# Transposing the query and key stacks of two heads at once

## What is computed

```python
x = x + 0.5 * ffn(layernorm(x))      # silu(x Wg^T) * (x Wu^T), then Wd^T; hidden 2048
q, k = unit_norm(q), unit_norm(k)    # per head; rotary embedding on every second head
logits = einsum(q, k) * q_gain       # causal mask, softmax
x = x + (softmax(logits) @ v) @ w_out
x = x + 0.5 * ffn(layernorm(x))
```

## Time and profile before

| | us |
|---|---|
| median of 3 runs | 2894.09 (2892.12 to 2894.12) |
| the profiled execution | 2897.56 |
| its span | 2895.8 |
| PE busy | 2765.8 (96%) |
| DVE busy | 1773.8 (61%) |
| ACT busy | 1193.0 (41%) |
| POOL busy | 535.8 (19%) |

### The profile page before, as it was taken

The page is one execution under the profiler, slowest core; times in us unless marked ns, Lnnn a source line. Parts: engine busy times, 40 slices in busy tenths (PEclk is TensorE's granted clock), DMA queues, the critical chain, the costliest instruction groups (busy, mean ns, idle before and its releaser), DMA issues.

```text
span 2895.8 us, 56172 instructions
## 1 busy us (share of the span) xinstructions
PE 2765.8 (96%) x23232; PEld 2029.6 (70%) x23232; DVE 1773.8 (61%) x4156; ACT 1193.0 (41%) x2218; POOL 535.8 (19%) x820
## 2 busy tenths in 40 slices
PE   4699989999999999999999999999999999998899
PEld 4467666777767776777767777677767777676676
DVE  8655766656566565666656666565656656566643
ACT  5233544444433443344433445344433443445422
POOL 0103122112030311203012131212103030123100
PEclk8899999999999999999999999999999999999999
DMA  6000000000000000000000000000000000000000
GB/s 249 15 1 1 1 1 1 16 1 16 1 1 16 16 1 1 1 16 16 1 1 1 16 16 2 1 16 9 9 1 1 16 16 1 1 1 9 1 9 15
DMA packets 15486, 37.28 MB, mean 13 GB/s; under 512 B 1408, under 2 KB 1408, under 8 KB 14720
## 3 DMA queue, kind: packets, MB, share of 16 engines
q1 hardware_dynamic: 15232, 33.70, 3.2%
HBM read 25.31 MB, written 8.39 MB: 12 GB/s over the span
## 4 chain that ended last, share of the span: by engine, by line
PE 84%; DVE 10%; ACT 3%; issue 2%; POOL 1%; DMA 0%; SPq 0%; DVEq 0%; ACTq 0%
PE psum L906 24%; PE psum L908 24%; PE psum L907 24%; PE psum L1055 2%; PE psum L1032 2%; PE psum L1067 1%; DVE mneg L820 1%; PE psum L1014 1%; DVE arena L841 1%; PE psum L949 1%; PE psum L1010 1%; DVE arena L768 1%; DVE arena L770 1%; PE psum L1033 1%; DVE arena L763 1%
## 5 line engine op out<-in xcount | busy, mean ns | idle before, releaser
L906 PE MATMUL psum<-arena,WG 128*128 128x256 f16 x2048 | 559.9, 273 | 1.4 <-DVE arena L763 1.4
L908 PE MATMUL psum<-arena,WG 128*128 128x256 f16 x2048 | 559.8, 273 | 0.0
L907 PE MATMUL psum<-arena,WG 128*128 128x256 f16 x2048 | 559.6, 273 | 0.0
L906 PE MATMUL psum<-arena,WU 128*128 128x256 f16 x2048 | 559.1, 273 | 0.0
L908 PE MATMUL psum<-arena,WU 128*128 128x256 f16 x2048 | 558.8, 273 | 0.0
L907 PE MATMUL psum<-arena,WU 128*128 128x256 f16 x2048 | 558.8, 273 | 0.0
L768 DVE SCALAR_TENSOR_TENSOR arena<-arena,psum 128x256 f32<-128x256 f32 x512 | 214.8, 420 | 529.1 <-ACT arena L643 528.1
L643 ACT ACTIVATE arena<-psum,tscale 128x256 f32<-128x256 f32 x512 | 241.8, 472 | 671.8 <-PE psum L908 671.7
L906 PE MATMUL psum<-WD,arena 128*128 128x512 f16 x1024 | 388.6, 379 | 12.7 <-DVE arena L774 12.7
L908 PE MATMUL psum<-WD,arena 128*128 128x512 f16 x1024 | 388.5, 379 | 0.0
L907 PE MATMUL psum<-WD,arena 128*128 128x512 f16 x1024 | 388.4, 379 | 0.0
(11 more groups left out here) (139 smaller groups left out, 4543.1 us busy)
## 6 DMA issues: line engine op xcount, KB each, us to landing
arena<-in_L_attn_x SPq DMA_DIRECT2D x16, 512.0 KB, 3.6
out<-arena SPq DMA_DIRECT2D x16, 512.0 KB, 2.8
arena<-in_L_ffn_w_gate SPq DMA_DIRECT2D x4, 1024.0 KB, 9.2
arena<-in_L_ffn_w_up SPq DMA_DIRECT2D x4, 1024.0 KB, 8.3
WD<-in_L_ffn_w_down SPq DMA_DIRECT2D x4, 1024.0 KB, 10.6
arena<-in_L_attn_w_qkv SPq DMA_DIRECT2D x1, 3072.0 KB, 20.6
WQ<-in_L_attn_w_out SPq DMA_DIRECT2D x1, 1024.0 KB, 22.8
ropet<-rope_table SPq DMA_DIRECT2D x1, 128.0 KB, 2.1
```

The source lines that it names most:

```text
L906: T_.matmul(o, lhs(0), rhs(0), start=first, stop=False)
L907: T_.matmul(o, lhs(0), rhs(1), start=False, stop=False)
L908: return T_.matmul(o, lhs(1), rhs(0), start=False, stop=last)
```

## The change

The query stack of a head is now written as (high, low) only, and the key stack as (low, high): 64 columns a head, so that two heads fill 128. One transpose turns two heads, 4 for the queries and 4 for the keys of a tile. In PSUM the even head lies on partitions 0 to 63 and the odd one on 64 to 127. Out of PSUM each group of four heads (even, odd) is copied twice: both parts to partitions 0 to 63 of QT or KT, and the high part once more to partitions 64 to 95. A query column is then (high, low, high) and a key column (low, high, high), which gives the same three products. One ScalarE instruction writes the high parts of all stacks.

```diff
-    STK = halves("work", 5 * D, HH * ST).rearrange("p (h c) -> p h c", h=2 * HH)
+    stk = halves("work", 5 * D, (2 * D + 2 * HD) // 2)
+    STQ, STK = (stk[:, D * a:D * (a + 1)].rearrange("p (h c) -> p h c", h=HH) for a in range(2))
+    SThi = stk.rearrange("p (a c) -> p a c", a=2)[:, :, 0:D].rearrange("p a (h c) -> p a h c", c=2 * HD)[:, :, :, 0:HD]
...
+    def stacked(key, odd):
+        bank = ps16(2 + key)[:, 0:D].rearrange("p (h n) -> p h n", n=P)
+        first = 2 * HD * odd
+        return bank[first + HD * key:first + HD * key + HD], bank[first:first + 2 * HD]
...
-                nc.scalar.activation(STK[:, :, 0:HD], q3, ACT.Copy)
-                nc.scalar.activation(STK[:, 0:HH, HD:2 * HD], q3[:, 0:HH, :], ACT.Copy)
-                nc.scalar.activation(STK[:, HH:2 * HH, 2 * HD:ST], q3[:, HH:2 * HH, :], ACT.Copy).then_inc(s["st_hi"], 1)
+                nc.scalar.activation(SThi, q3.rearrange("p (a h) c -> p a h c", a=2), ACT.Copy).then_inc(s["st_hi"], 1)
...
-                nc.scalar.activation(QT[0:ST, :, t * P:(t + 1) * P], ps16(2)[0:ST, :].rearrange("p (h n) -> p h n", h=HH),
-                                     ACT.Copy).then_inc(s["qt_ev"], 1)
+                for odd in range(2):
+                    high, both = stacked(0, odd)
+                    nc.scalar.activation(QT[0:2 * HD, odd::2, t * P:(t + 1) * P], both, ACT.Copy)
+                    ins = nc.scalar.activation(QT[2 * HD:ST, odd::2, t * P:(t + 1) * P], high, ACT.Copy)
+                ins.then_inc(s["qt_ev"], 1)
...
-                V_.tensor_copy(KT[0:ST, :, t * P:(t + 1) * P], ps16(3)[0:ST, :].rearrange("p (h n) -> p h n", h=HH)).then_inc(s["kt_ev"], 1)
+                for odd in range(2):
+                    high, both = stacked(1, odd)
+                    V_.tensor_copy(KT[0:2 * HD, odd::2, t * P:(t + 1) * P], both)
+                    ins = V_.tensor_copy(KT[2 * HD:ST, odd::2, t * P:(t + 1) * P], high)
+                ins.then_inc(s["kt_ev"], 1)
...
-                for h in range(HH):
-                    ins = T_.transpose(ps16(2)[0:ST, h * P:(h + 1) * P], STK[:, h, :], ident16[:, :])
+                for m in range(HH // 2):
+                    ins = T_.transpose(ps16(2)[:, m * P:(m + 1) * P], stk[:, m * P:(m + 1) * P], ident16[:, :])
...
-                for h in range(HH):
-                    ins = T_.transpose(ps16(3)[0:ST, h * P:(h + 1) * P], STK[:, HH + h, :], ident16[:, :])
+                for m in range(HH // 2):
+                    ins = T_.transpose(ps16(3)[:, m * P:(m + 1) * P], stk[:, D + m * P:D + (m + 1) * P], ident16[:, :])
```

More of the change, by code:

```diff
@@ L806, in stack @@
                 q3 = qn[t % 2].rearrange("p (h c) -> p h c", c=HD)
-                V_.tensor_tensor(STK[:, 0:HH, 2 * HD:ST], q3[:, 0:HH, :], STK[:, 0:HH, 0:HD], ALU.subtract)
-                V_.tensor_tensor(STK[:, HH:2 * HH, HD:2 * HD], q3[:, HH:2 * HH, :], STK[:, HH:2 * HH, 0:HD], ALU.subtract).then_inc(s["st_lo"], 1)
+                V_.tensor_tensor(STQ[:, :, HD:2 * HD], q3[:, 0:HH, :], STQ[:, :, 0:HD], ALU.subtract)
+                V_.tensor_tensor(STK[:, :, 0:HD], q3[:, HH:2 * HH, :], STK[:, :, HD:2 * HD], ALU.subtract).then_inc(s["st_lo"], 1)
             def stack_out(b, hf, t):
                 wait("kt_ps", tile_no(b, hf, t) + 1)
-                V_.tensor_copy(KT[0:ST, :, t * P:(t + 1) * P], ps16(3)[0:ST, :].rearrange("p (h n) -> p h n", h=HH)).then_inc(s["kt_ev"], 1)
+                for odd in range(2):
[3 more added lines that the diff above has]
+                ins.then_inc(s["kt_ev"], 1)
             mnegv = mneg[:, :].rearrange("p (t h) -> p t h", t=TT)
```

## The result

The changed kernel takes 2905.95 us (median of 6 runs, 2903.62 to 2908.93) against 2894.11 before (6 runs): ratio 1.0041, 95% interval 1.0031 to 1.0052. It is 11.8 us slower, where 6.7 was forecast (2901, range 2884 to 2908).

A forecast was written before the change was run, and what follows sets the result against it. PE, with 84% of the chain that ended last, was taken as the bound, so new PE waits count. 6.6 lost in batches 1 to 6 plus 0.1 in batches 0 and 7 gave 6.7 slower: 2901 median, range 2884 to 2908.

The forecast's parts named there:

- the forecast's own case: All new copies on ACT and DVE held until the one before is done: 6.7 slower, 2901; chance 0.55.
- two of the rivals: ACT held in part or not, 2894 (chance 0.17), wholly in range; copies overlapping, 2883 (chance 0.18), at its edge.
- Transposes, 0.44 a tile: PE: 8 transposes replace 16 at 0.056 each, 28 us over 64 tiles if nothing else moved.
- Copies held at each change of partition: Four PSUM copies per engine, each waiting for its predecessor: ACT ends at +2.86 (before +1.67), DVE +2.42 (before +1.79).
- The rivals of overlap, on both engines or on ACT alone: Copies overlap on both engines: 2883, chance 0.18; ACT held in part or not, DVE fully: 2894, chance 0.17.
- Single rate: DVE copies on 64 or 32 partitions lose the double rate, 0.69 a copy: 2937; chance 0.05.
- Tile by tile: Batches 1 to 6: losses and gains at each tile's PE waits sum to 1.10 lost a batch, 6.6 in six.
- `scores max` at +2.96: t3: waits for the query copies; 0.75 lost in half 0, 0.41 in half 1.
- `down` at +3.88: t2, both halves: waits for L774, late behind the query copies and L649; +3.51 before, 0.37 lost each.
- `turn` at +2.52: t0 of half 0: L949 needs the key copies; +2.20 before, 0.32 lost.
- Batches 0 and 7: 0.1 give or take 3: First and last batch: 0.7 and 2.7 lost, 1.2, 0.7 and 1.4 gained, 0.1 lost in sum.
- a gain of 0.7: Fourth `scores max` of batches 0 and 7, behind 2677.26 at low clock: its 16 transposes take 1.73 and become half.

The follow-up runs named there:

- half_transposes: Kernel before, with only 4 of the 8 query and 4 of the 8 key transposes per tile, copies kept at full size: 2870.94 against 2893.55, ratio 0.9924.
- split_heads: Kernel before, each copy out of PSUM made in four by heads, all of 96 partitions from and to partition 0: 2897.69, ratio 1.0015.
- split_partitions: Kernel before with its 16 transposes, each copy out of PSUM made in four with the changed kernel's sizes and partition changes: 2938.56, ratio 1.0157.
- queries_only: Kernel before with the change on the queries alone (4 transposes, four ACT copies), keys as before: 2904.54, ratio 1.0040.
- before_order: Kernel before, in half 0 last stack turn one fill earlier, feed-forward parts ahead of the copies and of unit: 2894.43, ratio 0.9995.
- sbuf_keys: Changed kernel with the keys' high parts copied the second time within SBUF instead of out of PSUM: 2898.05, ratio 1.0008.

## Why the prediction was right, and where it was too small

The measured 2905.95 lies in the stated range and in the narrower one of the forecast's own case (2897 to 2907), 5 above the forecast. The stated range takes in two of the rivals, so the time alone does not tell them apart; the rows below do.

- *Transposes, 0.44 a tile.* Right: 8 in 0.45. The count of tiles where it is gained whole was right too, with one miss: t3 of half 1 gains half of it (half_transposes).
- *Copies held at each change of partition.* Right on both engines. ACT was to start at +0.42 and end at +2.86: +0.42 and +2.82. DVE +0.65 to +2.42: +0.64 to +2.37. The rivals of overlap, on both engines or on ACT alone, fall with split_heads beside split_partitions. Single rate falls too: each copy on DVE took 0.42. With the rule of the Trainium skill, page "VectorE: DVE Perf Modes", section "Two Vector instructions with no wait between them", that an instruction whose input or output starts in another group of 32 partitions waits for all earlier ones, the DVE rows of these runs agree. The Trainium skill, page "ScalarE: Activation LUTs", section "What ACT_TABLE_LOAD costs", has back-to-back ACTIVATEs overlap by some 93 ns: split_heads shows about 110, and where the first partition changes there is no overlap (0.01 behind the end).
- *Tile by tile.* `scores max` at +2.96: measured +2.88 and, in half 1, +3.02. In half 1 it was the key copies that it waited for last (0.60), and not the query copies as the prediction has it: the key transposes stood 0.33 behind the normalisation's L773. The 0.10 given for the semaphore and for the break in PE's stream was 0.06 behind ACT's copies and 0.14 behind DVE's. `down` at +3.88: +3.77. `turn` at +2.52: +2.53. Stretches: 0.75, 0.41, 0.37 twice, 0.32 lost; measured 0.67, 0.47, 0.27 twice, 0.35. Gains 0.24 and 0.44 twice: measured 0.24 and 0.45 twice. Sum 1.10 a batch, measured 0.92; six batches 6.6, measured 5.55.
- *Batches 0 and 7: 0.1 give or take 3.* Measured 4.8 (3.90 + 0.86): this is the term that was too small. Three parts of it show. In batch 7, half 0, `turn` waited 1.20 for `norm` on DVE, which stood behind `gated`, and that behind ACT's four query copies: 1.18 lost between t0 and t1 (1.17 in queries_only), a loss that the sum does not list:

```profile
2541.05 0.47 ACT L653 ACTIVATE arena<-psum,tscale 128x256 f32<-128x256 f32 x1
...
2542.35 0.54 DVE L768 TENSOR_SCALAR arena<-arena,mv,rstd 128x512 f32<-128x512 f32 x1
...
2542.95 0.66 PE L963 MATMUL psum<-ident,arena 128*128 128x128 f32 x4 [1.20 <-DVE arena L768]
```

Behind the last `scores max` of batch 0 PE waited 0.6 longer for the row maxima, in the heads stage, where the prediction had expected no wait to grow. And in batch 0 the granted clock fell twice, which I had put at nothing. Stretches of the changed kernel, then the same work of the kernel before (the seventh number behind the span is PEclk):

```profile
393.50:397.00 3.50, 2.73 (x15) 1.83 (x16) 3.42 (x9) 0.35 (x1) 0.00 (x0) 0.69 0.00 0
434.50:438.00 3.50, 2.72 (x15) 1.75 (x16) 2.17 (x5) 2.38 (x4) 0.29 (x1) 0.69 0.00 0
```

```profile
392.50:396.00 3.50, 3.29 (x31) 2.51 (x32) 3.40 (x9) 0.00 (x0) 0.00 (x0) 1.00 0.00 0
431.20:434.70 3.50, 2.70 (x36) 2.18 (x37) 2.19 (x5) 2.47 (x4) 0.29 (x1) 1.00 0.02 5
```

PE runs part of both stretches at the lower level (1.2 GHz) and comes out 1.6 and 1.7 later, 3.3 in all. Ahead of the first it had stood idle for 0.97 at `scores max` and 1.06 for the next head's row maxima within 3 us. Without these 3.3 and the 1.05 of scatter ahead of the first tile the spans differ by 7.0, against the 6.7 forecast.

That this is so close is in part luck, for two errors cancel: the six middle batches came out 1.05 below their term and the two others 1.4 above theirs. And the comparison leans on a chance event in the other profile. The kernel before has a stretch of low clock in its own profile, behind 2677, on which the prediction builds a gain of 0.7. The run before_order does the same work there at full clock and is 1.57 shorter between that `stack turn` and `scores max`:

```profile
2676.40:2679.40 3.00, 2.79 (x33) 2.46 (x34) 2.09 (x6) 1.32 (x2) 0.00 (x0) 1.00 0.00 0
```

Against it the changed kernel does not gain there but loses 0.64, as at the `scores max` of half 0, and with full clock there on both sides the change costs 8.6 and not 7.0 (estimate from these numbers). The forecast took off the 3.5 by which the profiled execution lay above the median and kept that gain. If the executions at the median ran at full clock there, as before_order (2894.43) did, this accounts for 1.3 of the 5 us by which the median lies above the forecast. A second stretch, in the second head of batch 7 (behind 2721 before, behind 2733 after), is in both profiles and cancels.

What brings the low clock on stays open: queries_only has a like wait at the last `scores max` of batch 0 (0.74, then 1.05) and kept the full clock, split_heads fell once behind 387, at a `stack turn` that had waited 1.98, where the kernel before (1.79 at that place) did not. The six runs of the changed kernel form two groups, 2903.6 to 2904.4 and 2907.5 to 2908.9, and the median lies between them; the profiled execution is of the upper one. That the lower ones had no such stretch is likely, but no profile of one was taken.

## What to carry to other kernels

Count what comes out of PSUM before packing what goes in: halving the transposes saved 0.45 us of PE a tile, and four copies for one took 1.2 and 0.6 longer on the engines behind it. Copies whose first partition changes from one to the next (0, 32, 64, 96 here) lost their overlap of some 0.1, on ScalarE and VectorE both. A second placement of the same data was cheaper from SBUF than from PSUM (0.42 for 1024 elements against 0.84), and freed the bank earlier. When a producer gets faster and its evacuation slower, look for other work to put between the copies and their first reader; here that, with the copy inside SBUF and in half 0 alone, turned 0.4% slower into 0.4% faster.

## What the runs showed of the hardware

- An ACT instruction whose first partition differs from that of the one before starts 0.01 to 0.03 behind its end; with one first partition it starts 0.10 to 0.13 before it (split_heads, the kernel before). On DVE: 0.01 to 0.03 behind, against 0.08 before. A changed output is enough on ACT (L622 and L623 of the changed kernel), a changed input on DVE (L823 of sbuf_keys).
- Float16 transposes of 128 x 128 follow each other at 0.056 as those of 128 x 96 do (the changed kernel and the one before).
- A DVE copy of 32 partitions x 1024 float16 within SBUF takes 0.42, as one of 64 x 512 out of PSUM (sbuf_keys).
- A DVE instruction of 0.43 (L784) took 0.67 to 0.68 in the 14 places of sbuf_keys where POOL went over from L521 to L522 beside it, and L522 took 0.63 instead of 0.44.
- Kernels whose prologue is the same reach the first `stack turn` up to 3.6 us apart (235.5 to 239.0 in 14 traces).
